# Four resident graph layers on one core: summing each pass in two halves of the columns

## The chip, the cores and the metric

The kernel runs on one core of a Trainium2 chip. The time is device microseconds of one execution; before the change three runs took 1774.22, 1776.38 and 1778.61 us, median 1776.38.

PE (TensorE) multiplies into PSUM (8 banks of 512 columns), VectorE (DVE), ScalarE (ACT) and GpSimd (POOL) do the rest, and SP issues the transfers. Each has its own queue of instructions and executes it in order; semaphores are the only link between them.

## The reference, cut to what matters

`x` is 4096 x 128 and `adj` 4096 x 4096, all in float32. LN is a layernorm without weights.

```
x = LN(x + adj @ (f2 * (adj @ (relu(adj @ (f1 * (adj @ (x @ W1)))) @ W2))))   # passes 0 to 3
P = softmax(beta * (x @ x.T) / (|x| |x|.T + 1e-7) + (1 - adj) * -1e9)
x = LN(x + P @ x)                                                              # attention
msg = relu((adj @ x) @ W_msg.T + b_msg)                                        # pass 4
x = LN(x + GRU(msg, x))
x = LN(x + x @ W_self + ((adj @ x) / max(rowsum(adj), 1)) @ W_neigh)           # pass 5
```

The kernel computes `(adj @ x) @ W1` in place of `adj @ (x @ W1)`.

## The kernel before, in words

**A pass.** Each product with `adj` is one of six passes (0 to 5). `x` (or what stands for it) lies in 32 blocks of 128 rows; block b is the stationary operand, split into a rounded high part `yH` and the rest `yL`. The transposed `adj` comes in 64 tiles of 128 rows and 2048 columns, 1 MB each; tile (b, h) holds half h of the columns for block b. A tile is split too: ScalarE rounds it to `aH` (line 432), VectorE writes `aL = raw - aH` (line 686), both in two buffers. PE then multiplies `yH aH`, `yL aH`, `yH aL` (lines 1007, 1009, 1014), four matmuls of 512 columns each, into the four banks of half h. The tiles alternate between the halves, h = 0, 1, 0, 1, ..., so all eight banks fill until the last tile. PE's passes are a loop of four tiles (`tiles` in `multiply`). GpSimd copies the weights of each block from `yH`, `yL` to `wH`, `wL` (lines 348, 349).

`raw` is a ring of four tiles; SP loads a tile when the split of the tile four before it in the ring is done. Eight tiles of 64 (`KEPT_AT`) stay in SBUF for passes 0 to 3, and again eight for passes 4 and 5.

**Between passes.** When the last tile is done, ScalarE copies the eight banks out (line 445, then as `xT`), PE projects each by a weight or transposes it (lines 1030, 1032), VectorE applies the filter (line 704), ScalarE rounds to `yH` (line 435), VectorE makes `yL` (line 690). After pass 3 VectorE adds the residual (line 796), takes statistics (line 719), works out mean and scale in small steps (`scale_step`, with a square root of ScalarE, line 471), writes unit rows (line 806), which PE transposes and ScalarE and VectorE split into `unitH`, `unitL` in the space of `aH`, `aL`.

**Attention.** 16 blocks of two rows of 128: scores, mask with row maximum (line 836, VectorE), exponential (line 497, ScalarE), transposes, and the weighted sum. GpSimd turns a row of `adj` into a bias (line 376). The first block also normalises and splits `x` (`X_NORMALISED_AT`, `X_SPLIT_AT`); the last one normalises `x` again (line 782) and transposes it (line 1038).

**GRU and the end.** After pass 4, for each of eight chunks of 512 columns: message (line 1156), gates (lines 1168, 1169), the two parts of the new state (lines 1185, 1188), a transpose (line 1163); VectorE mixes. Then normalisation, splits, transposes and the own share (line 1201), and pass 5. Beside pass 5 GpSimd adds own share and row (`residual`, line 398). After it all columns are projected, scaled by the row sum on ScalarE (line 647), added (line 980), normalised by VectorE and ScalarE (lines 782, 464) and stored.

The order on each engine is written out by hand.

Of the kernel before, what the change touches and what calls it, by code (L numbers as in the profile page):

```python
# [37 lines left out]
def build(nc, x_rows, adjT, adj, early, late, norms, out):  # L50
# [5 lines left out]
    SPAN = NB // 2  # L56
    KEPT_AT = tuple(range(0, 2 * SPAN, 8))
    NKEPT = 2 * len(KEPT_AT)
    RING = 4
    TILES = 2 * NB  # L60
# [4 lines left out]
    FIRST, SECOND = (0, 1), (1, 2)  # L65
    LEAD = 4
    BY_ACT_LAST = (1, 3, 5, 7)
    SCALE_STEPS = 8
    EARLY_LN = NB - BPB

    X_NORMALISED_AT = {0: 6, 1: 7}
    X_SPLIT_AT = {3: 2, 4: 3, 5: 4, 7: 5, 9: 6, 11: 7}
    HIGH_BY_DVE = (1, 7, 11, 15)

    early_at, early_width = columns_of(EARLY, NB)
    late_at, late_width = columns_of(LATE, NB)

    with ExitStack() as ctx:
# [19 lines left out]
        split_base = next_base()  # L98
        aH = sb("aH", [D, 2, HALF], F32R)
        aL = sb("aL", [D, 2, HALF], F32R)  # L100
        kept = sb("kept", [D, 4, N])
# [7 lines left out]
        scratch = sb_over("scratch", [D, 10, BANK], F32, split_base)  # L109
        s1 = sb("s1", [D, 2 * NB])  # L110
        s2 = sb("s2", [D, 2 * NB])
        s3 = sb("s3", [D, 2 * NB])
# [13 lines left out]
        bsum = sb("bsum", [D, 2])  # L126
        ps = ctx.enter_context(nc.psum_tensor("ps", [D, 8, BANK], F32))

        def p(name, a=0, b=None):

            t, (at, w) = (par, early_at[name]) if name in EARLY else (lpar, late_at[name])
            return t[:, at + a:at + (w if b is None else b)]

        ident = p("ident")
        kept_tile = [kept[:, n // 2, (n % 2) * HALF:(n % 2 + 1) * HALF] for n in range(NKEPT)]
# [3 lines left out]

        gT0, z0 = [[xT[:, i * BANK:(i + 1) * BANK] for i in slots] for slots in (range(BK - 2), range(BK - 2, BK))]  # L140

        msg_s, r_s, z_s, n_s, g_s = [[scratch[:, 2 * i + j, :] for j in range(2)] for i in range(5)]
# [6 lines left out]

        BY_ACT = [k for k in range(NBATCH) if k not in HIGH_BY_DVE]  # L150

        def chunk(t, c):

            return t[:, c * BANK:(c + 1) * BANK]


        par_landed = sem("par_landed")
        x_landed = [sem(f"x_landed{h}") for h in range(2)]
        late_landed = sem("late_landed")
        tile_landed = [sem(f"tile_landed{s}") for s in range(RING)]  # L160
        kept_landed = [sem(f"kept_landed{k}") for k in range(NKEPT)]
# [4 lines left out]
        w_ready = sem("w_ready")  # L166
# [9 lines left out]
        act_norm_ready = sem("act_norm_ready")  # L176
        last_ready = sem("last_ready")
        scaled_ready = sem("scaled_ready")
# [4 lines left out]
        unit_ready = sem("unit_ready")  # L183
# [3 lines left out]
        unorm_ready = sem("unorm_ready")  # L187
# [38 lines left out]
        gru_step = sem("gru_step")  # L226
        gru_ready = sem("gru_ready")
        self_ready = sem("self_ready")
        sum_ready = sem("sum_ready")
        gruT_done = sem("gruT_done")  # L230
# [3 lines left out]
        block = ctx.enter_context(nc.Block())  # L234

        def rounds(eng, n, peel):

            yield from range(peel)
            if n > peel:
                with eng.Fori(peel, n) as it:  # L240
                    yield it
# [7 lines left out]
        def wait_bank(eng, pass_index, b):  # L249

            h, j = divmod(b, HBK)
            if j == HBK - 1:
                eng.wait_ge(tile_used, (pass_index + 1) * TILES - 1 + h)
            else:
                eng.wait_ge(bank_done, pass_index * (BK - 2) + h * (HBK - 1) + j + 1)


        @block.sync
        def _(sp):
            adjT_tiles = adjT.rearrange("(b q) (h c) -> b h q c", q=D, h=2)  # L260
            adj_rows = adj.rearrange("(b q) c -> b q c", q=D)
            streamed = [(k, h) for k in range(SPAN) for h in range(2) if 2 * k + h not in KEPT_AT]

            def load_kept(which):

                for n in which:
                    it, i = divmod(n, len(KEPT_AT))
                    b, h = divmod(2 * SPAN * it + KEPT_AT[i], 2)
                    sp.dma_start(kept_tile[n], adjT_tiles[b, h]).then_inc(kept_landed[n], 16)

            def stream(ps_index):

                base = ps_index * TILES
                for it in rounds(sp, 2, 2 if ps_index in (0, 4) else 0):
                    for s, (k, h) in enumerate(streamed):
                        if ps_index == 4 and (it, s) == (0, RING):

                            sp.wait_ge(pv_done, NSB * NBATCH)
                            load_kept(range(NKEPT // 2, NKEPT))
                            sp.dma_start(lpar[:], late).then_inc(late_landed, 16)  # L280
                        if ps_index == 0 and (it, s) in kept_before:
                            load_kept([kept_before[it, s]])
                        if ps_index == 0 and (it, s) == (0, RING):
                            sp.dma_start(par[:], early).then_inc(par_landed, 16)
                        before = s - RING
                        k0, h0 = streamed[before]
                        count = 2 * k0 + h0 + 1 - (2 * SPAN if before < 0 else 0)
                        if not (ps_index == 0 and isinstance(it, int) and it == 0 and before < 0):

                            sp.wait_ge(aL_ready, it * (2 * SPAN) + (base + count))  # L290
                        sp.dma_start(raw[:, s % RING, :], adjT_tiles[it * SPAN + k, h]).then_inc(tile_landed[s % RING], 16)


            kept_before = {divmod(n * len(streamed) // len(KEPT_AT), len(streamed)): n for n in range(1, NKEPT)}
            for h in range(2):
                cols = slice(h * HALF, (h + 1) * HALF)
                sp.dma_start(xrow[:, cols], x_rows[:, cols]).then_inc(x_landed[h], 16)
                if h == 0:
                    load_kept([0])
            for q in range(4):  # L300
                stream(q)
# [7 lines left out]
            sp.wait_ge(u_written, 16)  # L309
            sp.dma_start(xT[:, 0:N], norms.rearrange("b d -> (b d)").partition_broadcast(D)).then_inc(urow_landed, 16)  # L310
# [3 lines left out]

# [3 lines left out]

            sp.wait_ge(m_ready, NB * NCH)
            sp.wait_ge(pt_ready, (NSB - 1) * NBATCH)  # L320
            load_kept(range(NKEPT // 2))
            stream(4)
            stream(5)
            out_blocks = out.rearrange("(b q) d -> q b d", q=D)
            by_dve = [c for c in range(BK) if c not in BY_ACT_LAST]
            for c in sorted(range(BK), key=lambda c: (by_dve if c in by_dve else BY_ACT_LAST).index(c)):

                if c in BY_ACT_LAST:
                    sp.wait_ge(last_ready, BY_ACT_LAST.index(c) + 1)
                else:  # L330
                    sp.wait_ge(x_ready, HBK + 2 * BK + by_dve.index(c) + 1)
# [3 lines left out]


# [906 lines left out]
```

## Time and profile before

| | |
|---|---|
| median of 3 runs | 1776.38 us |
| span of the profiled execution (first to last instruction) | 1770.8 us |
| PE busy | 1666.0 us, 94% |
| VectorE busy | 1440.4 us, 81% |
| ScalarE busy | 1243.5 us, 70% |
| GpSimd busy | 402.4 us, 23% |
| moved from HBM | 441 MB, mean 250 GB/s |

The profile gives the span but not the execution's time outside it; the median lies 5.6 us above the span. PE's busy time counts modelled ends of pipelined matmuls, so that it says when PE had something to do, not at what rate it worked. The granted clock is 1.00 in the passes and lower where PE had stood still.

### The profile page before, as it was taken

To read this page: it belongs to the slowest core of one execution; us is meant where nothing else is said; L and a number is where in the kernel's file an instruction comes from. 1 tells how busy PE (TensorE), PEld (TensorE's weight loads), DVE (VectorE), ACT (ScalarE), POOL (GpSimd) and SP (SyncE) were. 2 spreads that over 40 slices of the span, in tenths; PEclk is the share of its full clock that TensorE was granted. 3 is DMA by queue.
4 is the path that set the end of the run, shared out by engine and by line. 5 is a ranking of instruction groups with operands and counts; after the bars stand their busy time and mean duration, and the time that the engine had idled before them with its cause. 6 is when DMAs were issued, how large, how long until landed. Compare 5 with 4: busy or idle time off the path is not lost.

```text
span 1770.8 us, 26215 instructions
## 1 busy us (share of the span) xinstructions
PE 1666.0 (94%) x8529; PEld 1391.4 (79%) x8529; DVE 1440.4 (81%) x1537; ACT 1243.5 (70%) x1220; POOL 402.4 (23%) x589
## 2 busy tenths in 40 slices
PE   7999999999998999869999999999979999799995
PEld 6888788888887888748888988899868886378884
DVE  7888888888888888888877777778788886888886
ACT  6677677677776777668777777777656776376666
POOL 1111121111111211233323333333012110023420
PEclk9999999999999999969999999999989999999998
DMA  9999699879996988733333333333368985049983
GB/s 396 387 386 383 242 349 338 336 273 343 338 338 223 345 337 338 294 143 108 136 139 139 128 118 139 143 142 142 153 257 331 344 339 205 1 171 332 332 332 113
DMA packets 60372, 444.26 MB, mean 251 GB/s; under 512 B 6368, under 2 KB 10624, under 8 KB 10752
## 3 DMA queue, kind: packets, MB, share of 16 engines
q1 hardware_dynamic: 60288, 443.36, 66.5%
q8 instruction: 25, 0.41, 0.1%
q14 instruction: 59, 0.48, 0.1%
HBM read 441.23 MB, written 2.11 MB: 250 GB/s over the span
## 4 chain that ended last, share of the span: by engine, by line
PE 81%; DVE 10%; ACT 4%; issue 3%; DMA 2%; DVEq 0%; POOL 0%; SPq 0%; ACTq 0%; POOLq 0%
PE ps L1014 18%; PE ps L1007 18%; PE ps L1009 18%; PE ps L1083 5%; PE ps L1098 3%; PE ps L1100 3%; PE ps L1099 3%; PE ps L1067 3%; PE ps L1069 3%; PE ps L1068 3%; DVE aL L686 2%; ACT aH L432 2%; DVE ptL L854 2%; DMA raw<-adjT 1%; DVE xrow L782 1%
## 5 line engine op out<-in xcount | busy, mean ns | idle before, releaser
L686 DVE TENSOR_TENSOR aL<-raw,aH 128x2048 fp32r<-128x2048 f32 x336 | 776.3, 2315 | 139.9 <-ACT aH L432 139.1
L432 ACT ACTIVATE aH<-raw 128x2048 fp32r<-128x2048 f32 x336 | 645.8, 1922 | 269.0 <-PE ps L1009 236.2
L1007 PE MATMUL ps<-aH,wH 128*128 128x512 f32 x1536 | 414.4, 392 | 13.2 <-ACT aH L432 10.4
L1014 PE MATMUL ps<-aL,wH 128*128 128x512 f32 x1536 | 413.3, 391 | 4.2 <-DVE aL L686 3.5
L1009 PE MATMUL ps<-aH,wL 128*128 128x512 f32 x1536 | 412.8, 391 | 0.0
L348 POOL CAST wH<-yH 128x128 fp32r (+1 forms) x192 | 146.3, 762 | 988.1 <-PE ps L1014 809.9
L1007 PEld LDWEIGHTS ps<-aH,wH 128*128 128x128 f32 x1536 | 289.1, 189 | 74.4 <-POOL wL L349 10.4
L1014 PEld LDWEIGHTS ps<-aL,wH 128*128 128x128 f32 x1536 | 287.8, 188 | 69.6 <-DVE aL L686 10.4
L1009 PEld LDWEIGHTS ps<-aH,wL 128*128 128x128 f32 x1536 | 289.9, 189 | 60.8
L854 DVE TENSOR_TENSOR ptL<-ps,ptH 128x512 fp32r<-128x512 f32 x256 | 176.6, 690 | 75.1 <-ACT ptH L505 72.5
L376 POOL TENSOR_SCALAR raw<-raw 128x2048 f32<-128x2048 f32 x64 | 122.6, 1916 | 306.9 <-ACT raw L490 306.7
L505 ACT ACTIVATE ptH<-ps 128x512 fp32r<-128x512 f32 x192 | 114.4, 596 | 103.3 <-PE ps L1083 98.8
L836 DVE CUSTOM_DVE_ANT_0 kept<-ps,raw 128x1024 f32<-128x1024 f32 x128 | 155.9, 1218 | 28.7 <-issue 22.3
L1098 PE MATMUL ps<-ptH,yH 128*128 128x256 f32 x512 | 150.6, 294 | 20.3 <-DVE ptL L854 18.6
L1083 PE MATMUL ps<-par,kept 128*128 128x128 f32 x1024 | 155.4, 275 | 0.0
L497 ACT ACTIVATE kept<-kept,nmax 128x1024 f32<-128x1024 f32 x128 | 145.9, 1142 | 0.7 <-DVE nmax L840 0.7
L1100 PE MATMUL ps<-ptH,yL 128*128 128x256 f32 x512 | 145.2, 284 | 0.0
L1099 PE MATMUL ps<-ptL,yH 128*128 128x256 f32 x512 | 144.4, 282 | 0.0
L1098 PEld LDWEIGHTS ps<-ptH,yH 128*128 128x128 f32 x512 | 97.5, 190 | 46.1 <-DVE ptL L854 35.5
L686 DVE TENSOR_TENSOR aL<-kept,aH 128x2048 fp32r<-128x2048 f32 x48 | 110.0, 2293 | 26.8 <-ACT aH L432 26.8
L1067 PE MATMUL ps<-aH,wH 128*128 128x512 f32 x256 | 123.3, 482 | 5.3 <-DVE cmax L836 5.2
L490 ACT ACTIVATE raw<-raw 128x2048 f32<-128x2048 f32 x64 | 122.1, 1909 | 0.5 <-DMA raw<-adj 0.4
(122 smaller groups left out, 1556.0 us busy)
## 6 DMA issues: line engine op xcount, KB each, us to landing
raw<-adjT SPq DMA_DIRECT2D x336, 1024.0 KB, 5.6
raw<-adj SPq DMA_DIRECT2D x32, 2048.0 KB, 7.8
kept<-adjT SPq DMA_DIRECT2D x16, 1024.0 KB, 7.6
xrow<-x_rows SPq DMA_DIRECT2D x2, 1024.0 KB, 7.1
xT<-norms SPq DMA_DIRECT2D x1, 2048.0 KB, 6.9
out<-xrow SPq DMA_DIRECT2D x8, 256.0 KB, 3.2
lpar<-late SPq DMA_DIRECT2D x1, 576.0 KB, 11.8
par<-early SPq DMA_DIRECT2D x1, 228.0 KB, 16.8
```

Source lines behind the costliest of these rows:

```text
L432: nc.scalar.activation(aH[:, h, :], src, ACT.Copy).then_inc(aH_ready, 1)
L686: dve.tensor_tensor(aL[:, h, :], src, aH[:, h, :].bitcast(F32), ALU.subtract).then_inc(aL_ready, 1)
L836: dve.tensor_tensor_reduce(kept[:, slot, c * CH:(c + 1) * CH], S2[c % 2], rowbuf[:, r, c * CH:(c + 1) * CH], 1.0, LOWEST, ALU.add, ALU.max ...
L854: dve.tensor_tensor(ptL[:, k % 2, :], ps[:, PT_BANKS[k % 2], :], ptH[:, k % 2, :].bitcast(F32), ALU.subtract).then_inc(ptL_ready, 1)
L1007: pe.matmul(b, wH[:, r, :], aH[:, h, c], start=first and r == 0, stop=False)
L1009: ins = pe.matmul(b, wL[:, r, :], aH[:, h, c], start=False, stop=False)
L1014: ins = pe.matmul(b, wH[:, r, :], aL[:, h, c], start=False, stop=done)
L1067: pe.matmul(o, wH[:, r, :], unitH[:, col], start=True, stop=False)
L1083: ins = pe.transpose(ps[:, PT_BANKS[k % 2], (2 * a + r) * D:(2 * a + r + 1) * D], kept[:, 2 * parity + r, j * D:(j + 1) * D], ident)
L1098: pe.matmul(o, yH[:, jc], ptH[:, k % 2, cols], start=(j == 0), stop=False)
L1099: pe.matmul(o, yH[:, jc], ptL[:, k % 2, cols], start=False, stop=False)
L1100: ins = pe.matmul(o, yL[:, jc], ptH[:, k % 2, cols], start=False, stop=(j == NB - 1))
```

## The change

Each pass goes through the 32 tiles of columns 0 to 2047 first, then through the 32 of the others. Four banks of PSUM are therefore finished when the second half begins. What follows a pass (copy, projection, filter, statistics, unit rows, GRU, normalisation, splits) is done for the finished half between the tiles of the other half, and for the second half between the first tiles of the next pass; `GRU_AT`, `NORM_AT`, `HIGH_AT`, `TURN_AT` and `SELF_AT` say behind which tile. PE takes its weights from `yH` and `yL` themselves and its passes are written out tile by tile; the weight copies go. GpSimd makes `yL`, the unit rows (half of those of the second half are VectorE's), most normalisations, the carried part of the GRU (`z * h`) and the residual of the last layer. The GRU mixes `(1 - z) * n + z * h` with a third sigmoid for `1 - z`. Passes 4 and 5 keep four tiles each 16, not eight. The first transfer of `x` is 512 columns. At the end the last four chunks are normalised by VectorE (two), ScalarE (one) and GpSimd (one); the row sum scales in VectorE's addition.

```diff
-    KEPT_AT = tuple(range(0, 2 * SPAN, 8))
+    KEPT_FIRST = tuple(range(0, TILES, 8))
+    KEPT_SECOND = tuple(range(0, TILES, 16))
+    X_LOADS = ((0, 1), (1, HBK), (HBK, BK))
+    GRU_AT = ((2, 5, 8, 11), (0, 2, 4, 6))
+    NORM_AT = ((11, 17), (8, 12))
+    HIGH_AT = ((14, 15, 20, 21), (11, 12, 15, 16))
+    TURN_AT = (17, 19, 21, 23)
+    SELF_AT = (19, 21, 23, 25)
...
@ gpsimd
-                        pool.tensor_copy(wH[:, r % 2, :], yH[:, bass.ts(b, D)].bitcast(F32))
-                        pool.tensor_copy(wL[:, r % 2, :], yL[:, bass.ts(b, D)].bitcast(F32)).then_inc(w_ready, 1)
+            def low(split, c, src):
+                pool.wait_ge(yH_ready, split * BK + c + 1)
+                pool.tensor_tensor(chunk(yL, c), src, chunk(yH, c).bitcast(F32), ALU.subtract).then_inc(yL_ready, 1)
+            for c in range(BK):
+                low(0, c, chunk(xrow, c))
+            for q in range(3):
+                for c in range(BK):
+                    low(q + 1, c, filtered[c % HBK])
+            pool.wait_ge(rstd_ready, 1)
+            for c in range(HBK):
+                unit(c)
+            for c in range(HBK):
+                pool.wait_ge(unit_by_pool, c + 1)
+                normalise(c, x_ready)
+                if c >= 1:
+                    low_of_x(4, c - 1, c)
...
+            for h in range(2):
+                for c in range(h * HBK, (h + 1) * HBK):
+                    gru_carried(c)
+                for g in (2 * h, 2 * h + 1):
+                    normalise_pair(g)
+                for c in range(h * HBK, (h + 1) * HBK):
+                    residual(c)
@ scalar, passes 1 to 3
+                for t in range(TILES):
+                    split_high(q, t)
+                    if t < 2 * HBK and t % 2 == 1:
+                        turned_sums(q - 1, HBK + t // 2, ACT.Relu if q - 1 == 1 else ACT.Copy)
+                    if 6 <= t < 6 + 2 * HBK and t % 2 == 0:
+                        high_of_filtered(q - 1, HBK + (t - 6) // 2)
...
+                        if 20 <= u < 20 + 2 * HBK and u % 2 == 0:
+                            unit_high((u - 20) // 2)
+                        if 23 <= u < 23 + 2 * HBK and u % 2 == 1:
+                            c = (u - 23) // 2
+                            act.wait_ge(tile_used, 3 * TILES + NB + BPB * (c + 1))
+                            high_of_x(c + 1, c)
@ vector, GRU beside the tiles
+            def gru_steps(h, u):
+                for i in range(HBK):
+                    c = h * HBK + i
+                    if u == GRU_AT[h][i] + 4:
+                        gru_rows(c)
+                    if u == GRU_AT[h][i] + 3:
+                        gru_argument(c)
+                        gru_mix(c)
+                    if u == GRU_AT[h][i] + 5:
+                        bank_stats(c, BK + c + 1)
@ tensor
-                tiles(0, True, False)
-                with pe.Fori(1, NB // 2 - 1) as it:
-                    tiles(it, False, False)
-                tiles(NB // 2 - 1, False, True)
+            for q in range(4):
+                for t in range(TILES):
+                    tile(q, t)
+                    if q >= 1 and 2 <= t < 2 + 2 * HBK and t % 2 == 0:
+                        project(q - 1, HBK + (t - 2) // 2, weights_of[q - 1])
+                    u = t - NB
+                    if 2 <= u < 2 + 2 * HBK and u % 2 == 0:
...
+                        project(q, (u - 2) // 2, weights_of[q])
+                    if q == 3 and 19 <= u < 19 + 2 * HBK and u % 2 == 1:
...
+                        unit_turn(c)
...
+            for t in range(TILES):
+                tile(4, t)
...
+                if 6 <= t < 6 + 2 * BK and t % 2 == 0:
+                    turn_chunk((t - 6) // 2, (t - 6) // 2)
...
+                if t >= NB:
+                    gru_steps(0, t - NB)
+            for t in range(TILES):
+                tile(5, t)
+                if t < NB:
+                    gru_steps(1, t)
```

## Rows read from the trace of the kernel before

**Rows 1.** Busy time by stretch: start and end, length, then each engine's us (instructions), clock, DMA
```profile
10.40:187.30 176.90, 176.68 (x768) 145.56 (x769) 149.05 (x68) 126.51 (x72) 30.68 (x60) 1.00 0.98 391
187.30:374.20 186.90, 182.69 (x835) 151.52 (x834) 157.04 (x80) 131.54 (x81) 35.76 (x64) 1.00 0.84 315
374.20:555.50 181.30, 181.30 (x833) 150.95 (x832) 151.64 (x72) 130.70 (x81) 30.92 (x64) 1.00 0.86 324
555.50:742.10 186.60, 181.74 (x801) 149.51 (x800) 157.04 (x80) 130.72 (x81) 33.55 (x64) 0.98 0.83 311
742.10:774.40 32.30, 16.00 (x74) 12.10 (x73) 28.60 (x101) 14.76 (x22) 8.14 (x12) 0.60 0.31 126
774.40:1297.50 523.10, 497.48 (x3367) 446.13 (x3365) 407.41 (x762) 391.20 (x616) 166.10 (x182) 0.98 0.37 137
1297.50:1310.50 13.00, 5.56 (x22) 4.90 (x23) 9.87 (x32) 9.36 (x16) 2.34 (x4) 0.65 0.91 365
1310.50:1484.70 174.20, 174.20 (x765) 143.54 (x764) 146.06 (x67) 122.88 (x69) 32.54 (x60) 1.00 0.89 332
1484.70:1565.10 80.40, 65.94 (x240) 36.61 (x240) 61.67 (x141) 40.00 (x63) 1.53 (x4) 0.94 0.04 13
1565.10:1743.00 177.90, 177.04 (x771) 143.43 (x770) 151.30 (x64) 124.08 (x70) 58.33 (x68) 1.00 0.84 307
1743.00:1770.80 27.80, 7.31 (x65) 7.11 (x63) 17.96 (x69) 16.40 (x53) 0.00 (x0) 0.72 0.27 76
```

**Rows 2.** Chain (first row) and PE's timeline: a projection; one GRU chunk between two transposes
```profile
374.21 7.14 PE ps L1032 x64
...
1500.37 0.60 PE L1163 MATMUL ps<-par,scratch 128*128 128x128 f32 x4
1500.81 1.02 PE L1156 MATMUL ps<-xrow,lpar 128*128 128x512 f32 x2
...
1506.82 0.60 PE L1163 MATMUL ps<-par,scratch 128*128 128x128 f32 x4
```

**Rows 3.** VectorE's timeline after pass 3: first scale step, first unit rows, first mask
```profile
753.85 0.21 DVE L732 TENSOR_TENSOR s<-par 128x32 f32<-128x32 f32 x1
...
758.11 3.17 DVE L806 TENSOR_SCALAR kept<-xrow,mean,s 128x128 f32<-128x128 f32 x12
...
774.35 1.23 DVE L836 CUSTOM_DVE_ANT_0 kept<-ps,raw 128x1024 f32<-128x1024 f32 x1 [1.65 <-PE ps L1069]
```

**Rows 4.** Timeline at the end: first scale step, ScalarE's normalisations
```profile
1757.60 0.22 DVE L732 TENSOR_TENSOR s<-par 128x32 f32<-128x32 f32 x1
...
1760.65 6.26 ACT L464 ACTIVATE xrow<-xrow,shift,rstd 128x128 f32<-128x128 f32 x16 [1.70 <-DVE shift L776]
```

**Rows 5.** Groups by line: busy us, mean ns of one, idle before
```profile
L365 POOL TENSOR_SCALAR par<-par 128x128 f32<-128x128 f32 x32 | 12.1, 377 | 6.5 <-POOL par L363 6.3
L398 POOL TENSOR_TENSOR xrow<-xrow,xT x8 | 10.3, 1286 | 0.0
L704 DVE TENSOR_TENSOR xT<-ps,par 128x512 f32<-128x512 f32 x16 | 10.9, 690 | 1.6 <-PE ps L1030 0.5
L868 DVE SCALAR_TENSOR_TENSOR xrow<-ps,rsum,xrow 128x128 f32 x24 | 7.3, 347 | 1.9 <-DVE rsum L863 1.9
```

**Rows 6.** VectorE's tile splits from 1480 to 1745 us: min/median/max ns
```profile
L686 DVE TENSOR_TENSOR aL<-raw,aH x58: 2278/2293/3367, 1477.9 to 1739.6; 128x2048 fp32r<-128x2048 f32 x58
```

**Rows 7.** Timeline in pass 5: GpSimd's residual addition, VectorE's splits behind it
```profile
1600.24 1.28 POOL L398 TENSOR_TENSOR xrow<-xrow,xT  x1
...
1600.59 5.29 DVE L686 TENSOR_TENSOR aL<-raw,aH 128x2048 fp32r<-128x2048 f32 x2 [0.70 <-ACT aH L432]
```

**Rows 8.** Timeline at pass 1's start: VectorE's splits, GpSimd's weight copy beside them
```profile
202.01 6.78 DVE L686 TENSOR_TENSOR aL<-raw,aH 128x2048 fp32r<-128x2048 f32 x3
...
206.60 2.35 POOL L349 CAST wL<-yL 128x128 fp32r x1
```

**Rows 9.** ScalarE's timeline before a square root: loading its function table
```profile
1540.15 1.28 ACT L471 ACT_TABLE_LOAD   x1
```

**Rows 10.** The chain in the attention where VectorE's loop starts over
```profile
889.39 3.26 issue
```

More of the change, by code:

```diff
@@ L259, in _ @@
+        @block_ctx.sync
         def _(sp):
-            adjT_tiles = adjT.rearrange("(b q) (h c) -> b h q c", q=D, h=2)
+            adjT_tiles = adjT.rearrange("(b q) (h c) -> h b q c", q=D, h=2)
             adj_rows = adj.rearrange("(b q) c -> b q c", q=D)
[L262 to L291, printed above, removed]
@@ L294, in _, with load_kept @@
[L294 to L299, printed above, removed]
-            for q in range(4):
-                stream(q)
+            def load_kept(q, t):
+                n = kept_tiles(q).index(t)
+                sp.dma_start(kept_tile[n], adjT_tiles[t // NB, t % NB]).then_inc(kept_landed[n], 16)
@@ L883, in super_block @@
                 for k in range(NBATCH):
-                    if not before and k in X_NORMALISED_AT:
-                        normalise(X_NORMALISED_AT[k])
-                    if not before and k in X_SPLIT_AT:
-                        low(X_SPLIT_AT[k], chunk(xrow, X_SPLIT_AT[k]), 4)
                     m = (k + LEAD - 2) // 2
@@ new lines, in last_rows @@
+            def last_rows(c):
+                dve.wait_ge(proj_done, 4 * BK + c + 1)
+                dve.wait_ge(sum_ready, c + 1)
+                for i in range(BPB):
+                    b = c * BPB + i
+                    t = block(xrow, b)
+                    ins = dve.scalar_tensor_tensor(out=t, in0=ps[:, c, i * D:(i + 1) * D], scalar=rdeg[:, b:b + 1], in1=t,
+                                                   op0=ALU.mult, op1=ALU.add)
+                ins.then_inc(t_ready, 1)
+            dve.wait_ge(rdeg_ready, 1)
@@ new lines, in own_share @@
+            def own_share(c):
+                pe.wait_ge(xT_ready, BK + c + 1)
+                pe.wait_ge(zg_ready, (c // HBK + 1) * HBK)
+                pe.wait_ge(t_ready, BK + (c // HBK + 1) * HBK)
+                if c % HBK >= 2:
+                    pe.wait_ge(self_ready, c - 1)
+                for i in range(BPB):
+                    ins = pe.matmul(ps[:, self_bank[c], i * D:(i + 1) * D], chunk(xT, c)[:, i * D:(i + 1) * D], p("Ws"), start=True, stop=True)
+                ins.then_inc(self_done, 1)
@@ L1207 @@
+            for t in range(TILES):
+                tile(5, t)
+                if t < NB:
+                    gru_steps(1, t)
+                u = t - NB
+                if 3 <= u < 3 + 3 * HBK and u % 3 == 0:
+                    last_share((u - 3) // 3)
+            for b in range(HBK, BK):
+                last_share(b)
 NAMES = ("x_rows", "adjT", "adj", "early", "late")
```

1065 lines of the change are left out of this document (596 added, 469 removed).

## The prediction, before the run

> **What bounds the kernel now.** I read the stage table first: the span cut at the last matmul of each pass [rows 1]. Compare PE's busy time with each stretch's length. Inside a pass PE is busy all the time: pass 4 is one unbroken 174.2 us, 2.72 per tile of 64. The three stretches that hold a pass and the gap before it take 186.9, 181.3 and 186.6, so the gaps 0-1, 1-2, 2-3 are 12.8, 7.2 and 12.5 us. The long gaps are elsewhere: 32.3 us after pass 3 until the first mask, 13.0 after the attention, 80.4 between passes 4 and 5, 27.8 at the end. Second I read the order of instructions in those gaps, since PE's own work in them stays, wherever it is put. Summed over the table PE is busy 1666 us of 1760: the ceiling of any overlap is near 100 us. Third come the prices of what VectorE and GpSimd do beside a tile.
>
> **What stays on PE.** A projection of all columns by a weight is 7.14 us [rows 2], 0.89 per chunk of 512 columns; the pure transposes of a chunk take 0.44 (start 1500.37 to 1500.81). One GRU chunk repeats every 6.45 us and PE works through it without a hole [rows 2]: seven matmuls at 0.86 and one chunk of transposes. The change drops none of this; it puts it between tiles.
>
> **The sum**, as changes of the profiled execution (span 1770.8; the median of the runs shown is 5.6 longer, which I carry as a constant). First what happens if nothing moved makes a tile late:
> - Start: a smaller first load lets the first tile begin earlier, but tile 4 still waits for the same bytes, and DMA is 98% busy in pass 0 [rows 1]. -1 (0 to -5).
> - Gaps 0-1, 1-2, 2-3: 32.5 us become projections, 7.15 + 7.15 + 3.65: -14.5. What ScalarE and VectorE do for them fits beside the tiles, where pass 4 leaves ScalarE (174.2 - 122.9) / 64 = 0.80 and VectorE 0.44 us idle per tile [rows 1].
> - End of pass 3: half of its projection and half of the unit transposes come in, eight chunks at 0.44: +3.6.
> - After pass 3: today 11.75 us until the statistics of 8 chunks are done, 4.26 for the scales, 16.2 for units, transposes and splits until the first mask [rows 3]. With half the chunks left I get 6.6, 4.3 and 8.1: first mask after 19.0 us, -13.3. The first attention block also loses two normalisations and six splits on VectorE, -1.5 of its 32 us. Together -14.8 (-8 to -20).
> - Last attention block: VectorE loses seven normalisations but gains two tile splits (2.29 each [rows 6]), ScalarE two roundings: +2.5 (0 to +5).
> - After the attention: the 13.0 us go; eight chunks of transposes, 3.5, and 0.3 of start stay: -9.2.
> - Between passes 4 and 5: 80.4 go; 8 x 6.45 + 8 x 0.44 + 8 x 0.89 = 62.2 stay: -18.2. The GRU's own chain hides today behind 6.45 us of PE work a chunk; in the new order two or three tiles, 5.4 or 8.2 us, stand beside it as well, so PE should not wait for it.
> - Pass 5: its 177.9 are 3.7 above pass 4, for eight additions of GpSimd; they move: -3.7. Half of the last projection comes in: +3.6.
> - SP's queue: passes 4 and 5 keep 4 tiles instead of 8 in SBUF and stream 60, 7% more bytes in passes that grow by a third; pass 4 moves 332 GB/s now, pass 0 391 [rows 1]. The store of the norms now waits for projection and unit transposes and no tile load stands behind it before the masks. 0.
> - The end: today 14.6 us to the statistics of 8 chunks, 3.0 for scales, 6.3 for the normalisation, 3.9 from there to the end [rows 4]. Four chunks are left, with four scaled additions of 0.35 for one of 0.69 [rows 5], so about 2.3 a chunk: 1.5 + 9.1 + 3.0 + 2.5 + 3.9 = 20.0, -7.8.
> Sum: -59.5, hence 1717.
>
> **What the moved work costs beside tiles.** GpSimd loses the 384 weight copies. Beside tiles it gets about 49 operations of 512 columns (24 splits of yL in passes 1 to 3, 4 in pass 3, 5 in pass 4, 8 behind the GRU, 8 residuals) and some 96 of 128 columns (units, normalisations); 16 more fall where the GRU waits for its gates. The nearest prices are 1.29 and 0.37 us [rows 5]. VectorE splits a tile in 2.29 us, at worst in 3.37 [rows 6], and a case stands in the trace [rows 7]: a GpSimd addition runs from 1600.24 to 1601.52, the split that begins at 1600.59 waits for it, and two splits take 5.29. So a large operation takes up to 1.07 us from VectorE, and pass 5 lost 3.7 / 8 = 0.46 for each: some 0.6 is reserve. The small ones seem free for VectorE: three splits back to back take 6.78 while a weight copy passes between them [rows 8]; but that copy took 2.35, so it waited for a whole split. GpSimd then gets one small operation per split, one or two per tile, and ScalarE, in order, waits for the result.
> The Trainium skill (SBUF — State Buffer, section "Who interferes with whom") says that a VectorE instruction with two SBUF inputs and a GpSimd instruction that reads SBUF exclude each other, whichever starts first blocking the other for its whole length. By that the small operations take 0.37 each from VectorE too; for the half of them in crowded stretches that is 18 us, and the sum would come to 1760. The three splits in 6.78 us speak against that price.
>
> Per crowded stretch I compare VectorE plus GpSimd with PE:
> - Passes 1 to 3, 24 large operations spread over tiles with projections: 0 to 24 x 0.46 = 11; I take 1.5, as no copies precede them now.
> - Pass 3 from tile 49: VectorE 15 x 2.29 + 4 x 0.69 = 37.1, GpSimd 32 x 0.37 + 4 x 1.29 = 17.0, together 54 against PE's 15 x 2.72 + 1.8 = 42.6. ScalarE's tile roundings stand in order behind roundings that wait for GpSimd. 0 to 14; I take 7.
> - Pass 4, tiles 2 to 18: 36.6 + 5.0 (scales [rows 3], two last rows) + 11.1 against 47.0. I take 6 (0 to 12).
> - Pass 4 from tile 47 and pass 5 from tile 10, behind the GRU, each: 13 x 2.29 + 6.0 + 16.2 = 52 against 40.8, less what overlaps; ScalarE also switches its function table, 1.28 a time [rows 9], between sigmoid and root. I take 4 each, 8 (0 to 20).
> - Second half of pass 5: 2.5 (0 to 5).
> Together 25: 1776.4 - 59.5 + 25 = **1742**.
>
> **Rivals.**
> A. PE hides everything; the crowded stretches cost nothing. For it: GpSimd is busy only 32.5 of pass 4's 174.2 us. Against it: the 0.46 of each addition in pass 5. 1714 to 1724.
> B. GpSimd becomes the bound of the passes, and the kernel is slower. Place: GpSimd normalises, ScalarE rounds the result, GpSimd subtracts, and that rounding stands in ScalarE's order between tiles. Price: all of GpSimd's moved work exposed, 49 x 1.29 + 96 x 0.37 = 99 us, 1717 + 99 = 1816; slower than before once 60 of the 99 are exposed. For it: a copy that waited 2.35. Against it: while PE stands still VectorE runs dry too, and then GpSimd is free, so that the chain cannot stay blocked.
> C. PE's passes are a loop of four tiles today and become 4608 matmuls in a row; their code could come late. The trace shows such idle time, 3.26 us, where the attention's loop starts over [rows 10], once per two blocks, some 840 PE instructions (3367 matmuls with their weight loads in 16 blocks). At that rate 9216 / 840 = 11 times 3.26 is 36: 1778, no change. Against it: within the two blocks PE runs without a hole, at more instructions per us than in a pass.
> D. The stalls are twice what I took: 1757 to 1771, still faster.
>
> **How the numbers follow.** Forecast, 1724 to 1757: 0.62. A 0.17, D 0.10, C 0.05, B 0.06. The range goes from no stalls to double: 1714 to 1768; it leaves out some 0.05 below and 0.12 above. 0.3% of 1776 is 5.3 us, about what a measurement of this kernel tells from no change: faster (below 1771) 0.62 + 0.17 + 0.10 = 0.89, within it 0.04, slower 0.07 (C split between the two).
>
> **What would show it.** From pass 0's last matmul to pass 1's 181 to 184 us, to pass 2's 179 to 182 more, and no PE idle where the gaps were. Pass 3's second half takes 94 to 101. The first mask comes 19 us after pass 3. From the last sum of the attention to pass 5's last matmul 430 to 440, today 445.5. The end is 19 to 21. VectorE's tile split has a mean above 2.4, and ScalarE's waits name GpSimd's xrow in passes 3 to 5. I am wrong if PE idles more than 50 us inside the passes (B or D), if idle time without a releaser shows on PE every few tens of us (C), or if the 32.3 us after pass 3 shrink by less than 8.

## The result, and the profile after

The change made the kernel slower: 1797.38 us, median of 4 runs (1796.48 to 1798.30), against 1775.30 (median of 4) for the kernel before beside it, a ratio of 1.013 (95% interval 1.011 to 1.0149). Forecast were 1742 us, range 1714 to 1768, and slower had a chance of 0.07. The profiled execution spans 1795.7 us, where the prediction's sum gives 1736.3 for it (1770.8 - 59.5 + 25).

The page of the kernel after, parts 1 and 4:

```profile
PE 1674.9 (93%) x8529; PEld 1391.3 (77%) x8529; DVE 1385.7 (77%) x1450; ACT 1230.2 (69%) x1179; POOL 537.6 (30%) x417
...
PE 74%; POOL 10%; DVE 6%; issue 4%; ACT 3%; DMA 2%; DVEq 0%; SPq 0%; POOLq 0%; ACTq 0%
```

GpSimd is busy for 30% of the span only, and yet 10% of the chain is its work. A share of busy time does not tell what ends last; the chain does.

The stage table of the kernel after answers to [rows 1], with the same columns (PE, PEld, DVE, ACT, POOL, clock, DMA, GB/s):

```profile
191.70:372.80 181.10, 181.10 (x832) 151.11 (x831) 152.78 (x73) 130.68 (x81) 23.63 (x8) 1.00 0.88 325
372.80:552.50 179.70, 179.70 (x818) 149.34 (x817) 153.40 (x73) 131.01 (x81) 23.62 (x8) 1.00 0.88 327
...
643.40:753.20 109.80, 95.69 (x410) 75.77 (x408) 81.38 (x72) 64.62 (x45) 62.09 (x43) 0.94 0.72 255
753.20:782.40 29.20, 9.66 (x45) 6.80 (x45) 14.12 (x51) 8.67 (x14) 10.89 (x12) 0.66 0.16 65
782.40:846.30 63.90, 50.52 (x290) 43.76 (x291) 38.59 (x66) 46.74 (x70) 39.27 (x45) 0.86 0.43 162
846.30:1318.50 472.20, 447.97 (x3060) 406.31 (x3059) 354.18 (x647) 340.75 (x529) 159.42 (x172) 0.98 0.37 134
1318.50:1430.80 112.30, 103.30 (x455) 82.57 (x455) 81.92 (x57) 74.41 (x55) 40.60 (x27) 0.98 0.81 296
1430.80:1551.70 120.90, 114.97 (x470) 83.01 (x469) 88.82 (x90) 79.72 (x68) 47.90 (x32) 0.99 0.67 240
1551.70:1639.20 87.50, 79.27 (x289) 53.97 (x288) 64.05 (x79) 55.50 (x52) 42.12 (x28) 0.96 0.58 199
```

Passes 1 and 2 are as forecast: PE is never idle in 181.1 and 179.7 us. Then come the stretches that lost: the second half of pass 3 (PE idle for 14 of 109.8 us), the way to the first mask, the first attention block, the attention, the first 34 tiles of pass 4, and what stands beside the GRU behind them. In one table (forecast: the prediction's terms laid on the marks of before; last column: the reordered kernel e8, below):

| stage | before | forecast | after | e8 |
|---|---|---|---|---|
| end of pass 3's last tile | 742.1 | 738.7 | 753.2 | 739.9 |
| to the first mask | 32.3 | 19.0 | 29.2 | 24.4 |
| to the first turned sums | 60.1 | 58.6 | 63.9 | 57.4 |
| to the last sum of the attention | 463.0 | 465.5 | 472.2 | 470.8 |
| to pass 5's last tile | 445.5 | 434.5 | 459.4 | 440.3 |
| the end | 27.8 | 20.0 | 17.8 | 17.9 |
| span | 1770.8 | 1736.3 | 1795.7 | 1750.7 |

What GpSimd does there, its groups by line (busy us, mean ns of one | idle before). They answer to L365 and L398 of [rows 5], from which the prediction priced them at 0.37 and 1.29 us:

```profile
L352 POOL TENSOR_SCALAR xrow<-xrow,mean,rstd 128x128 f32<-128x128 f32 x116 | 152.8, 1329 | 127.8 <-DVE rstd L820 127.7
L362 POOL TENSOR_SCALAR xT<-xrow,mean,s 128x128 f32<-128x128 f32 x24 | 32.3, 1358 | 108.4 <-DVE rstd L818 101.3 <-issue 7.1
L347 POOL TENSOR_TENSOR yL<-xrow,yH 128x512 fp32r<-128x512 f32 x32 | 69.0, 2165 | 62.9 <-ACT yH L489 62.9
```

And the two rows for L352's price alone, min/median/max in ns, first of the kernel after, then of run e1, whose form takes one scalar from memory:

```profile
L352 POOL TENSOR_SCALAR xrow<-xrow,mean,rstd x116: 782/792/5044, 716.7 to 1791.4; 128x128 f32<-128x128 f32 x116
```
```profile
L352 POOL TENSOR_SCALAR xrow<-xrow,rstd x116: 367/376/4632, 709.6 to 1746.6; 128x128 f32<-128x128 f32 x116
```

Read the minimum and the median first: in the form of the kernel after (subtract the mean, multiply by the scale, two scalars from memory) one costs 0.78 us, in that of e1 (multiply by the scale, add the constant 0.0) 0.37. The forms differ in their arithmetic as well as in their scalars, and no run separates the two. The count of scalars from memory is not the whole price: GpSimd's addition of a constant in the GRU has none and costs 1.49 us for 512 columns, per column about what e1's form costs.

```profile
L441 POOL TENSOR_SCALAR scratch<-scratch 128x512 f32<-128x512 f32 x8 | 11.9, 1493 | 168.8 <-ACT scratch L665 168.8
```

The mean of 1.33 holds waiting behind VectorE as well, about 0.5 in both forms (e1's mean is 0.84). Last, who waits for it, kernel after (total us, times, longest): ScalarE's rounding of the normalised rows, and TensorE behind it.

```profile
ACT yH L489 <- POOL xrow L352: 59.0, 18, 8.5
```
```profile
PE ps L1090 <- ACT aH L486: 25.8, 11, 8.5
...
PE ps L1127 <- POOL xT L362: 14.1, 3, 9.8
PE ps L1159 <- POOL wL L378: 11.7, 1, 11.7
PE ps L1090 <- ACT aH_end L486: 9.9, 2, 6.9
```

The chain in pass 3 can be read off three timelines (start, length): GpSimd makes 16 unit rows in 26.09 us and only then normalises; ScalarE has stood 8.52 us in its order for these rows, the next tile's rounding right behind; TensorE gets that tile 6.9 us late, and its next matmuls run at the lower level of the clock, 1.2 GHz: the granted clock is 0.50 from 722.3 to 727.0, and four of them take 2.07 us where they take 1.07 at 1.00.

```profile
690.60 26.09 POOL L362 TENSOR_SCALAR xT<-xrow,mean,s 128x128 f32<-128x128 f32 x16 [101.31 <-DVE rstd L818]
716.67 6.21 POOL L352 TENSOR_SCALAR xrow<-xrow,mean,rstd 128x128 f32<-128x128 f32 x8
```
```profile
719.88 0.63 ACT L489 ACTIVATE yH<-xrow 128x512 fp32r<-128x512 f32 x1 [8.52 <-POOL xrow L352]
720.41 1.89 ACT L486 ACTIVATE aH_end<-kept 128x2048 fp32r<-128x2048 f32 x1
```
```profile
722.36 2.07 PE L1090 MATMUL ps<-aH_end,yH 128*128 128x512 f32 x4 [6.90 <-ACT aH_end L486]
```

After pass 3 GpSimd stands 7.06 us with no releaser right behind its reduction over partitions, and the unit rows wait; 16 normalisations and four subtractions (787.76 on) are then ahead of the weights that the second row block needs (806.79):

```profile
766.31 0.38 POOL L408 PARTITION_ALL_REDUCE umax<-umax  x1 [5.83 <-PE ps L1127]
773.75 6.25 POOL L362 TENSOR_SCALAR xT<-xrow,mean,s 128x128 f32<-128x128 f32 x8 [7.06 <-issue]
...
787.76 6.23 POOL L352 TENSOR_SCALAR xrow<-xrow,mean,rstd 128x128 f32<-128x128 f32 x8
...
806.79 0.46 POOL L378 TENSOR_TENSOR wL<-par,wH 128x128 fp32r<-128x128 f32 x1 [0.19 <-POOL wH L376]
```

### The profile page after: what moved, and what is told of

It reads as the page before. It is cut to its first block, busy times and chain, and to the rows that moved or that the text cites. A ratio compares the mean times of both kernels' runs of the same rounds, so it can differ in the third digit from the quotient of the medians.

```text
span 1795.7 us, 23985 instructions
## 1 busy us (share of the span) xinstructions
PE 1674.9 (93%) x8529; PEld 1391.3 (77%) x8529; DVE 1385.7 (77%) x1450; ACT 1230.2 (69%) x1179; POOL 537.6 (30%) x417
## 4 chain that ended last, share of the span: by engine, by line
PE 74%; POOL 10%; DVE 6%; issue 4%; ACT 3%; DMA 2%; DVEq 0%; SPq 0%; POOLq 0%; ACTq 0%
PE ps L1096 16%; PE ps L1090 15%; PE ps L1092 15%; POOL xrow L352 7%; PE ps L1174 6%; PE ps L1189 3%; PE ps L1191 3%; PE ps L1190 3%; DVE aL L757 3%; PE ps L1159 3%; PE ps L1161 3%; PE ps L1160 3%; DMA raw<-adjT 2%; POOL xT L362 2%; ACT aH L486 2%
## 5 line engine op out<-in xcount | busy, mean ns | idle before, releaser
L1090 PE MATMUL ps<-aH,yH 128*128 128x512 f32 x1408 | 391.9, 400 | 25.8 <-ACT aH L486 25.8
L1096 PE MATMUL ps<-aL,yH 128*128 128x512 f32 x1408 | 382.1, 393 | 9.8 <-DVE aL L757 9.3
L1092 PE MATMUL ps<-aH,yL 128*128 128x512 f32 x1408 | 380.1, 392 | 0.0
L1090 PEld LDWEIGHTS ps<-aH,yH 128*128 128x128 f32 x1408 | 260.6, 189 | 88.7 <-issue 26.4
L1096 PEld LDWEIGHTS ps<-aL,yH 128*128 128x128 f32 x1408 | 263.8, 189 | 75.6 <-DVE aL L757 21.4
L1092 PEld LDWEIGHTS ps<-aH,yL 128*128 128x128 f32 x1408 | 266.4, 189 | 57.1
L347 POOL TENSOR_TENSOR yL<-xT,yH 128x512 fp32r<-128x512 f32 x24 | 71.2, 2968 | 434.9 <-ACT yH L489 434.9
L352 POOL TENSOR_SCALAR xrow<-xrow,mean,rstd 128x128 f32<-128x128 f32 x116 | 152.8, 1329 | 127.8 <-DVE rstd L820 127.7
L1159 PE MATMUL ps<-aH,wH 128*128 128x512 f32 x256 | 123.9, 484 | 14.5 <-POOL wL L378 11.7
L1174 PEld LDWEIGHTS ps<-par,kept 128*128 128x128 f32 x1024 | 121.6, 143 | 2.1
```

Source lines behind the costliest of these rows:

```text
L352: ins = pool.tensor_scalar(t, t, mean[:, b:b + 1], rstd[:, b:b + 1], ALU.subtract, ALU.mult)
L1090: pe.matmul(b, block(yH, k), high[:, c], start=(k == 0), stop=False)
L1092: ins = pe.matmul(b, block(yL, k), high[:, c], start=False, stop=False)
L1096: ins = pe.matmul(b, block(yH, k), low[:, c], start=False, stop=(k == NB - 1))
L1159: pe.matmul(o, wH[:, r, :], unitH[:, col], start=True, stop=False)
L1174: ins = pe.transpose(ps[:, PT_BANKS[k % 2], (2 * a + r) * D:(2 * a + r + 1) * D], kept[:, 2 * parity + r, j * D:(j + 1) * D], ident)
```

## The experiments

Theory B: GpSimd's chain (its operation at twice the price, ScalarE's and TensorE's order behind it) is the bound at five places. Rival L: the engines are simply full there. Edits are against the kernel after unless said otherwise and are cut to the lines that matter; comments in them are mine. The kernel before was measured again beside each group of runs (medians 1771.67 to 1775.30); "less" compares medians across these groups, and the ratios in brackets (95% interval) are each against the kernel before beside it.

**e1, the price.**
```diff
-ins = pool.tensor_scalar(t, t, mean[:, b:b + 1], rstd[:, b:b + 1], ALU.subtract, ALU.mult)
+ins = pool.tensor_scalar(t, t, rstd[:, b:b + 1], 0.0, ALU.mult, ALU.add)
```
(the unit rows alike; the mean is left out of both, so the output differs, while the count of operations stays)

> GpSimd's 128 normalisations and 24 unit rows take one scalar from memory and one constant, as line 365 of the kernel before does (377 ns); the mean is left out of them, so the numbers of the output differ. Theory P (GpSimd's chain became the bound because such an operation with two scalars from memory costs 0.79 us and not 0.38): the median of one operation falls to 0.38, the 16 unit rows of pass 3 take 9 to 14 us instead of 26.1, ScalarE's waits for GpSimd's rows fall from 59 us to under 20, and the time falls from 1797 to 1750 to 1765. Rival L (GpSimd waits behind VectorE's long splits, whatever its own operation costs): the mean of one stays over 1 us beside splits, the waits stay over 40 us and the time stays at 1788 or more. Rival I (the stalls come from the fetch of longer programs): no change, 1795 to 1800.

1757.12 us, 40 less than after, ratio to before 0.9906 (0.9885 to 0.9926). Median 0.376, and ScalarE's wait falls from 59.0 to

```profile
ACT yH L489 <- POOL xrow L352: 19.8, 7, 4.6
```
The second half of pass 3 takes 97.4 us, inside the 94 to 101 of the prediction:

```profile
643.40:740.80 97.40, 93.14 (x416) 73.63 (x414) 83.47 (x73) 65.82 (x47) 48.69 (x41) 1.00 0.81 291
```

The price is the main cause, and rival I of the expectation, which forecast no change, falls. What stays is e1's mean of 0.84 beside splits: part of L holds, as waiting, but it is not what made the kernel slower.

**e2, the rounding out of pass 3.**
```diff
-  if 23 <= u < 23 + 2 * HBK and u % 2 == 1: ... high_of_x(c + 1, c)
+for c in range(HBK): high_of_x(c + 1, c)      # behind unit_high of the last chunks
```
(GpSimd's four subtractions move with them, ahead of its last normalisations)

> The rounding and the subtraction of the first half's four normalised chunks (ScalarE, GpSimd) are moved from inside pass 3's last tiles to behind the pass; all work stays. Theory B (ScalarE, in its own order, waits for GpSimd's normalisation and so brings the next split late, line 489 waiting 8.5 us): pass 3's last matmul comes 10 to 17 us earlier after the same start, the first mask stays within 3 us of its distance from it, and the time falls to 1781 to 1788. Rival L (the second half of pass 3 is long since VectorE's and GpSimd's operations lengthen one another): the pass gives back under 4 us, 1793 or more. Third way: the moved operations lie on the path to the first mask or to the first sums, and what the pass gives back is lost there: 1792 to 1800.

1796.63 (1.0129, 1.0107 to 1.0152): nothing in sum, but both halves of the story show. Pass 3's closing transposes start at 741.09 instead of 753.20, the 12 us of theory B:

```profile
741.09 2.12 PE L1118 MATMUL ps<-par,xT 128*128 128x128 f32 x16
```

All of it is lost again: GpSimd's moved subtractions are now ahead of the staged weights too, and TensorE waits

```profile
PE ps L1157 <- POOL wL L378: 23.5, 2, 18.8
```
The third way of the expectation: a wait moved along GpSimd's queue, not removed.

**e3, the last unit rows on VectorE.**
```diff
-for c in (HBK, HBK + 1):          # VectorE; GpSimd made HBK + 2, HBK + 3
+for c in range(HBK, BK):
```


> The eight unit rows of the last two chunks are made by VectorE (8 x 0.34 us) and no longer by GpSimd behind its reduction over partitions; all work stays. Theory: the first mask comes 7 to 11 us earlier after the pass's last matmul (29.4 before; the 7.1 us that GpSimd stands behind the reduction and its 6.25 us of units go, 2.7 us of VectorE come), and the time falls to 1786 to 1790. Rival: the first mask waits for GpSimd's other work there (the adjacency bias, the staged weights) or for VectorE's flag behind the same reduction, and under 3 us is gained: 1794 to 1798.

1784.61 (1.0056, 1.0035 to 1.0077), 12.8 less than after. Closing transposes at 758.11, first mask at

```profile
776.33 1.22 DVE L888 CUSTOM_DVE_ANT_0 kept<-ps,raw 128x1024 f32<-128x1024 f32 x1
```
that is 18.2 us, 11 less than after and near the 19.0 that the prediction had (pass 3 itself ended 4.9 later in this execution than in after's). So it was GpSimd's 7.06 idle and 6.25 of units that kept the mask.

**e4, later dates behind the GRU.**
```diff
-HIGH_AT = ((14, 15, 20, 21), (11, 12, 15, 16)); TURN_AT = (17, 19, 21, 23); SELF_AT = (19, 21, 23, 25)
+HIGH_AT = ((16, 18, 23, 25), (13, 15, 19, 21)); TURN_AT = (18, 20, 24, 26); SELF_AT = (20, 22, 26, 28)
```


> Only the tiles at which ScalarE rounds, TensorE turns and projects the GRU's normalised rows are changed (2 to 5 tiles later), all work and every engine's amount stay. Theory B (ScalarE and TensorE stand in order for GpSimd's normalisation, 5 to 9 us for a chunk): the waits of line 489 for GpSimd's rows behind the GRU fall from about 27 us to under 8 and the time falls by 10 to 20 us, to 1777 to 1787. Rival L (the engines are full there, VectorE at 2.3 of 2.8 us a tile before the GRU's own work): under 4 us, 1793 to 1798. Third way: with dates so late the last chunks come too late for the next tiles that read them (yH and yL of tile 28 of pass 5), and the second half of the GRU gets slower: 1797 to 1805.

1789.41 (1.0086, 1.0065 to 1.0107), 8.0 less; a little under the range of theory B, twice L's. ScalarE's wait behind the GRU, 1427 to 1640 us, after and then e4:

```profile
ACT yH L489 <- POOL xrow L352: 18.1, 7, 6.3
```
```profile
ACT yH L489 <- POOL xrow L352: 7.7, 3, 4.0
```

**e5, the scales ahead of pass 4 a block earlier.**
```diff
-EARLY_LN = NB - BPB        # scales in the last attention block
+EARLY_LN = NB - 2 * BPB    # in the last but one; ScalarE rounds the last chunks at tiles 10 and 13
```


> Ahead of pass 4: the scales of the first 24 row blocks (not 28) are worked out one attention block earlier, so that GpSimd normalises six of the eight chunks while it would stand idle, and the last two beside tiles; ScalarE rounds chunks 6 and 7 at tiles 10 and 13 instead of 7 and 9. All work stays. Theory B (pass 4's first tiles wait for GpSimd's normalisations, about 4 us each through ScalarE's order): ScalarE's waits for GpSimd's rows between 1295 and 1345 us fall under 6 us, the third of the pass up to the first message gets 6 to 12 us shorter, time 1785 to 1791. Rival L (VectorE's splits and scales fill that stretch whatever GpSimd does): under 3 us, 1794 to 1799.

1784.65 (1.0055, 1.0037 to 1.0073), 12.7 less. The last sum to the first GRU message takes 100.7 us instead of 112.6 (1317.2 to 1417.9). ScalarE's wait there is 0.4 us where it was 13.6 (first e5, then after):

```profile
ACT yH L491 <- POOL xrow L352: 0.4, 1, 0.4
```
```profile
ACT yH L489 <- POOL xrow L352: 13.6, 4, 4.1
```

**e6, ScalarE normalises after pass 3.**
```diff
-    normalise(c, x_ready)                     # GpSimd, c in HBK..BK-1
+    ins = nc.scalar.activation(block(xrow, b), block(xrow, b), ACT.Identity, bias=shift[:, b:b + 1], scale=rstd[:, b:b + 1])
```


> After pass 3 ScalarE (idle there) normalises the last four chunks, 16 x 0.48 us, instead of GpSimd, whose 16 x 0.79 stand in its queue ahead of the weights that it stages for the second block of rows; TensorE waited 11.7 us for those weights in the kernel after. Theory Q (that queue is what makes the first attention block longer, 63.8 us from the first mask to the first turned sums against 60.1 before): the wait for the staged weights falls under 3 us and the time by 8 to 12, to 1785 to 1789. Rival: ScalarE's 7.7 us lie ahead of its exponentials and put the same time there; the wait goes and the time stays at 1793 to 1799.

1792.81 (1.0096, 1.0072 to 1.0120), 4.6 less. That lies between theory Q and the rival, and the interval overlaps that of the kernel after, so the time settles neither. The trace does show the wait for the staged weights halved, from 11.7 us to 5.5; the subtractions are still ahead of them.

```profile
PE ps L1166 <- POOL wL L378: 5.5, 1, 5.5
```

**e7, all five,** with the second block's weights staged ahead of the last subtractions.

> All together, whole computation: the roundings of the first half behind pass 3, the unit rows of the last four chunks on VectorE, the normalisation of these on ScalarE and the weights of the second block staged first, the scales ahead of pass 4 one block earlier, and the later dates behind the GRU. If the lost time was GpSimd's chain at five places (theory B), the gains add: pass 3 about 12, first mask 11, staged weights 9 to 12, start of pass 4 6 to 10, GRU 8 from the run with the later dates: 1797 - 46 to 53, so 1744 to 1753, faster than before. Rival L (the engines are full whatever the order): the single gains take from one another and it stays over 1765.

1757.22 (0.9900, 0.988 to 0.992): faster than before, 40 less than after, 4 above the range. The gains of the single runs add up (0.8 + 12.8 + 8.0 + 12.7 + 4.6 = 38.9), but one place falls short: the first mask is 27.9 us behind pass 3 (740.16 to 768.11), though the unit rows are on VectorE as in e3 (18.2). VectorE's timeline in e7 and GpSimd's beside it:

```profile
750.51 0.35 DVE L805 RECIPROCAL s<-s 128x32 f32<-128x32 f32 x1 [2.26 <-ACT s L503]
750.90 1.21 DVE L807 TENSOR_TENSOR s<-s 128x32 f32<-128x32 f32 x1
...
753.37 1.18 DVE L811 TENSOR_SCALAR s<-s 128x32 f32<-128x32 f32 x1
754.59 0.35 DVE L813 RECIPROCAL s<-s 128x32 f32<-128x32 f32 x1
...
756.64 1.87 DVE L816 COPY rstd<-s 128x16 f32<-128x16 f32 x1
```
```profile
749.55 4.96 POOL L347 TENSOR_TENSOR yL<-xrow,yH 128x512 fp32r<-128x512 f32 x4
754.60 3.88 POOL L384 TENSOR_SCALAR raw<-raw 128x2048 f32<-128x2048 f32 x2
```

The same VectorE steps take 0.19, 0.18 and 0.17 in e3, where GpSimd rests; the last of them there:

```profile
768.51 0.17 DVE L814 COPY rstd<-s 128x16 f32<-128x16 f32 x1
```

In e7 each ends with the GpSimd operation beside it, and the reciprocals stay at 0.35.

**e8, nothing of GpSimd's four subtractions beside the scales.**
```diff
-for c in range(HBK): low_of_x(4, c, c + 1)
 mask_bias(0, 0)
 ...                                            # the reduction over partitions
 mask_bias(1, 1)
+for c in range(HBK): low_of_x(4, c, c + 1)
```
(and ScalarE's row sums go ahead of its roundings)

> As the run with all five, but GpSimd's four subtractions of the first half stand behind its reduction over partitions, no longer beside VectorE's scales, and the row sums of the adjacency go ahead of the roundings on ScalarE. In the run with all five VectorE's scale steps of 0.17 to 0.43 us took 1.2 to 1.9 us each while GpSimd ran subtractions (1.24) and the bias (1.9). Theory X (an operation of GpSimd with two operands holds VectorE off for its whole length): those steps fall back to under 0.5 us, the first mask comes 17 to 21 us after pass 3's last matmul instead of 26, and the time falls by 5 to 8 to 1749 to 1752. Rival: VectorE's small steps are slow for another reason (their own chain), they stay over 1 us and the time stays at 1755 to 1759. Third way: the four subtractions now come too late for the staged weights or the first sums, and the gain is lost there.

1753.98 (0.9875, 0.9855 to 0.9895). First mask 24.4 us behind pass 3 instead of 27.9 (by the expectation's mark, the last closing transpose, 22.5 instead of 26.1). The steps that now stand alone are short again; the two beside the bias are not:

```profile
748.96 0.33 DVE L807 TENSOR_TENSOR s<-s 128x32 f32<-128x32 f32 x1
...
749.68 0.18 DVE L811 TENSOR_SCALAR s<-s 128x32 f32<-128x32 f32 x1
...
750.29 1.90 DVE L814 TENSOR_TENSOR unorm<-s 128x16 f32<-128x16 f32 x1
...
752.31 1.89 DVE L816 COPY rstd<-s 128x16 f32<-128x16 f32 x1
```
This speaks for theory X as the mechanism. As a forecast it came out short: the first mask was to come at 17 to 21 us, and the 3.2 us against e7 lie inside the intervals. About 2 us of the earlier mask come from the other part of the edit, ScalarE's order: VectorE's wait for the square root is 0.29 us instead of 2.26.

**e9, VectorE's attention loop written out** (on e8).
```diff
-with dve.Fori(0, (NSB - 4) // 2) as it:
+for it in range((NSB - 4) // 2):
```


> As the run before it, and VectorE's program of the attention's middle blocks is written out, without a loop; the other engines keep their loops. Theory: VectorE's start-over (3.7 to 4.1 us of idle time without a releaser, five times, after which TensorE's clock is at its lower level for some us) is the jump back in VectorE's own program; without it the five gaps go to under 0.5 us and the time falls by 15 to 25. Rival 1: another engine's loop (TensorE, ScalarE) has the same gap at the same place, hidden today: the gaps stay over 2 us and the gain is under 8. Rival 2: five times as much code for VectorE, with its conditional jumps, comes late all along: slower.

1728.72 (0.9738, 0.9716 to 0.9759), 25.3 less than e8, the fastest of all. The stretch around one start-over, e8 and then e9 (columns as in the stage table):

```profile
940.00:955.00 15.00, 12.47 (x79) 11.13 (x77) 8.18 (x15) 7.98 (x13) 2.57 (x2) 0.89 0.11 44
```
```profile
940.00:955.00 15.00, 15.00 (x109) 13.85 (x109) 11.66 (x24) 12.05 (x19) 5.41 (x6) 1.00 0.39 138
```
The gap is gone and with it the stretch at the lower clock.

**e10, e8 in e1's form.**

> The reordered kernel with GpSimd's normalisations and unit rows in the form with one scalar from memory (the mean is left out of these, so the numbers differ). In the kernel after, that form alone gave 40 us back. If the new order has taken GpSimd's chain off the path (theory B and its cure), the cheaper form gives under 8 us here. If GpSimd's price still sets the pace (rival: the order only moved the waits), it gives 15 or more.

1745.69 (0.9825, 0.980 to 0.9851): 8.3 less than e8, where the same edit gave 40 in the kernel after. A little above theory B's bound, far from the rival: the new arrangement took GpSimd's price off the path but for about 8 us. It is not the order alone, since 24 of GpSimd's 140 operations of this kind (8 unit rows, 16 normalisations) are now VectorE's and ScalarE's.

**e11, the kernel before with TensorE's passes written out.**
```diff
-with pe.Fori(1, NB // 2 - 1) as it:
+for it in range(1, NB // 2 - 1):
```


> The kernel before, and only TensorE's passes are written out instead of a loop of four tiles, as the change does. Rival C of the prediction (the code of a written-out pass comes late): each of six passes gets 3 to 8 us longer, with idle time on TensorE that has no releaser: 1790 to 1815. My theory: no idle time in the passes, 1772 to 1780. If the start-over of the attention's loop grows from 3.2 to about 3.8 us here too, the longer program is the cause of that growth; if it stays at 3.2, it is not.

1771.80 (0.9979, 0.9966 to 0.9993). Written-out passes cost nothing, so rival C falls; and the start-over of the attention is 2.8 to 3.1 us here, so the length of TensorE's program does not explain its growth.

**e12, the kernel before with e9's edit.**

> The kernel before, and only VectorE's loop of the attention's middle blocks is written out. It tells what of the 25 us of the reordered kernel with that loop written out belongs to the change. Theory: the start-over is VectorE's own and costs before as after, so five gaps of 3.2 us and the clock behind two of them go: 16 to 22 us, 1752 to 1759. Rival: the gaps cost much only in the new order (3.7 to 4.1 us, clock down behind four of them): under 10 us here, 1765 or more.

1756.09 (0.9908, 0.9885 to 0.9930), 15.6 less than the 1771.67 of before beside it, just short of the theory's range. So e9's gain is not the change's: the loop costs the kernel before 16 us and the reordered one 25. With the loop written out in both, the reordered change stands at 1728.72 against 1756.09 (0.9738 of the kernel before against 0.9908). The change as it was predicted was not run with the loop written out.

## Why the prediction was wrong

The failed step is "What the moved work costs beside tiles", and in it the price of the small operations of GpSimd: "The nearest prices are 1.29 and 0.37 us". 0.37 is L365 [rows 5], which multiplies by one scalar from memory and adds a constant; the normalisations and units subtract one scalar from memory and multiply by another, and cost 0.79 alone and 1.33 in the mean. I took the shape for the price and left the form of the operation out. Forecast stalls of 25 us became about 84 (25 and the 59.4 by which the span is above the sum), or 78 without the attention's loop. e1 has the price that I assumed: it takes 1757.12, inside the range, so the price stands for 40 of the 55 us by which 1742 was missed.

Of the signs named beforehand, the 32.3 us after pass 3 shrank by only 3.1, less than the 8 that I had set; PE idles some 41 us inside the passes (1.8 in pass 0, 14.1 in pass 3, 25.3 from the last sum to pass 5's last tile), under the 50; VectorE's split has a mean of 2.338 us, not above 2.4; ScalarE's waits name GpSimd's `xrow`, as forecast. Point by point, in the table's stages:

- Passes 1 and 2 with the gaps ahead of them: right, 181.1 and 179.7 us against 181 to 184 and 179 to 182. The end is 2.2 us shorter than the sum had it, 17.8 against 20.0.
- Pass 3: +14.5. I compared the sum of VectorE's and GpSimd's work with PE's. The right comparison is of one chain: 16 units in 26.09 us, then the normalisation, then ScalarE's rounding in ScalarE's order (the 8.52 us above). e1 gives 97.4 us for the half pass, e2 gives the 12 us back.
- First mask: +10.2. The term was right for the work (e3: 18.2), but I gave two chunks' units to GpSimd at no cost and did not see that its reduction is followed by 7 us without an instruction. In the kernel before the 6.73 us behind it ended with VectorE's split `aL` (L812), so GpSimd had to wait there anyway.
- First attention block: +5.3. GpSimd's normalisations are queued ahead of the weights it stages, and PE waits 11.7 us. The prediction did not name what is behind them in that queue.
- Attention: +6.7. In the middle blocks code and work are unchanged. VectorE's loop starts over in 3.75 to 4.07 us, before 3.12 to 3.26 [rows 10], five times, and PE's clock drops behind four of them instead of two (granted 0.72 to 0.86 in the 12 us behind these, 1.00 behind the others). The chain of the kernel after names the jump itself (L957 is the loop's line):

```profile
901.14 0.06 DVEq L957
901.21 3.75 issue
904.95 0.04 DVEq L957
```
 That this is VectorE's jump is shown (e9). Why it got longer is open: it is 3.7 to 4.1 in every kernel with the new passes that keeps the loop and 2.8 to 3.3 in both with the old passes.
- Last sum to pass 5's last tile: +24.9, of it about 10 ahead of the first message (e5 removes 12) and 15 behind it (e4 removes 7.4). e4 and e5 show the same chain for about 19 of it; the rest is not isolated. The pace that I took, "one small operation per split, one or two per tile", is too slow for four in a chunk and a subtraction behind them.

Rival B had place, order and turning point right: slower "once 60 of the 99 are exposed", and about 78 were, if the rest of the sum is taken as right. It got 0.06 because its price came from the same wrong row; with 0.79 its total is 49 x 1.29 + 96 x 0.79 = 139, and I would have given it several times that chance. My argument against it (when PE stands still GpSimd is free to catch up) is true of one stall, but the lower clock after a stall (0.50 above) and the next date in ScalarE's order came on top.

On the exclusion of VectorE and GpSimd I held three splits in 6.78 us [rows 8] against a price for VectorE. For splits that stood the test: their mean over all tiles is 2.315 us before and 2.338 after (in GpSimd's crowded stretches it is GpSimd that waits). It is false for VectorE's small steps beside GpSimd's large operations, 0.17 to 0.19 in e3 and up to 1.87 in e7. The Trainium skill (SBUF — State Buffer, section "Who interferes with whom") says that whoever starts first holds the shared ports for its whole instruction, and that VectorE needs them with two inputs in SBUF or in a mode that copies and `tensor_scalar` can enter. The trace agrees as far as it goes: L807 (two inputs), L811 and L816 (a `tensor_scalar`, a copy) were held, the reciprocals stayed at 0.35.

## What to carry to other kernels

Price an operation by a row with the same operands and the same arithmetic, not only the same shape and engine; where none is there, take the neighbouring form as one end and its double as the other. For work moved to a slow helper engine, write out the chain through the other engines' orders and what is queued behind it on the helper, since the same difference in price cost 40 us in one arrangement and 8 in another. Look at a loop's start-over too: writing it out gave 16 us in the kernel before, and the change lost 22.

## What the runs showed of the hardware that was not expected

- GpSimd, `tensor_scalar` of 128 x 128: 0.78 us for subtract and multiply with two scalars from memory, 0.37 for multiply and add with one and a constant. Which of the differences makes the price is not shown.
- GpSimd's reduction over partitions takes 0.38 us but has 5.71 and 6.22 us without an instruction ahead of it (e7, e8) and 7.06 and 6.91 behind it (after, e3). The Trainium skill (GPSIMD Engine Reference, section "2.1 Instruction dispatch") tells of about 6 us for the first call to freshly loaded code. The time ahead agrees; that the way back to ordinary operations costs as much is not said there, but the trace has two `MODIFY_POOL_CONFIG` records of GpSimd's queue ahead of the 7.06 us too (at 766.6).
- VectorE's jump back in a long loop: 2.8 to 4.1 us without an instruction, each time; it is gone where the loop is written out (e9, e12).
